# Attention in a graph network: the difference "product minus group maximum" formed by TensorE in PSUM instead of by VectorE in SBUF

## The chip, the cores and the metric

The kernel runs on one core of a Trainium2 chip, in one launch. The metric is the device time of that launch in microseconds (us), the median of several runs. The engines are called TensorE (PE in the rows; PEld are its weight loads), VectorE (DVE), ScalarE (ACT), GpSimd (POOL) and SyncE (SP). SBUF is the working memory of 128 partitions, PSUM the eight banks of 128 x 512 f32 into which TensorE writes.

## The reference

Four graph layers over 6250 nodes and 206,250 edges (sorted by destination) are applied one after the other to node rows x of 16 numbers. The change touches the fourth, an attention over the edges of each node:

```python
w_m = (efeat @ W_msg + b_msg).reshape(E, in_f, -1)      # 16 x 16 per edge
w_a = (efeat @ W_attn + b_attn).reshape(E, in_f, -1)
h_src = feat[src][:, :, None]
e1 = w_m * h_src
e2 = w_a * h_src
seg_max = jax.ops.segment_max(e2, dst, num_segments=N)
ex = jnp.exp(e2 - seg_max[dst])
denom = jax.ops.segment_sum(ex, dst, num_segments=N)
attn = ex / denom[dst]
ft = jax.ops.segment_sum(e1 * attn, dst, num_segments=N)
return ft.sum(axis=1)
```

## The kernel before

The fourth layer puts the edges of a node into quads of four; an edge that is missing is marked void. Each of the 128 partitions owns 440 quads (LQ), worked through in 110 blocks (NBQ) of QB = 4 quads, so a block holds 16 edges per partition. For each edge there are CH = 256 attention products and 256 message products. `walk` runs the first blocks unrolled, then a loop of two blocks per turn, then the last ones unrolled. The engines are ordered by semaphores written out by hand; `At(k)` is block k, `at.of(per, more)` a semaphore count for it, `turn_wait` a wait. Each engine works strictly in the order of its own program:

- SyncE loads the lines of two quads of each block and stores `S`, the maxima first (`keep_tops`, L2097 to L2099, when `s_sub` says so), the sums later (L2107).
- GpSimd gathers the 16 source rows of a block into `got` (L2127) and the lines of the other two quads (L2138).
- TensorE, in `step` (L2199): for block k it makes the matrices of block k+1, `matrices(at, q, half)` (L2171, L2178), two matmuls of K = 32 rows per half quad in different row groups, into PSUM `pw[half]`; the sums over the four edges of a quad of block k-1, `quad_sum` (L2181, L2186), four accumulating matmuls of the identity with `X[:, q, n, :]`, into `pq[q % 2]`; and the transposes of the lines of block k+2, `turned` (L2160, L2167), into `pturn`. The order in a step: matrices of quad 0, quad sums 0 and 1, matrices of quads 1 to 3, transposes, quad sums 2 and 3.
- VectorE, in `a_block` (L2299): `times` (L2272, L2281) multiplies `pw[half]` by the gathered row into `T[at.b]` (attention and message products of half a quad). For block k it takes the maximum over the four edges of each quad (L2324, L2327), carries it forward over the quads of the same node (`forward`, L2304) and back (`back`, L2309), each step depending on the one before. Between these steps stand the `times` of block k+1 (`ahead`) and the additions of quad sums of block k-1 to the running state (`add`, L2287, L2294). Then come the two subtractions of the maxima from `T` in place, one for each half of the block (L2343), each followed by `s_sub`; `drop` (L2345, L2346), the last `times`, two additions, the two products of `X` and the message part (L2356, waiting for `s_x`), and `carried` (L2359).
- ScalarE, in `step` (L2236): marks of void edges (L2230), the two exponentials from `T` to `X` (L2243) after `s_sub` and the quad sums of the block before (`X` is one buffer), the exponential of `drop` (L2245), the copy of the transposed lines from PSUM to `efT` (`features`, L2234), and indices (L2226).

`S[b]` holds maxima, sums and weighted sums of four quads. All of this is f32.

## Time and profile before

| what | value |
|---|---|
| median of 3 runs | 10060.28 us |
| lowest and highest | 10052.39, 10067.98 us |
| span of the profiled execution | 13003.9 us |
| in it, VectorE busy | 8219.9 us (63%) |
| TensorE busy | 8950.8 us (69%) |
| GpSimd busy | 6780.0 us (52%) |
| ScalarE busy | 2527.0 us (19%) |
| mean granted TensorE clock | 0.763 of full speed |

The profile is one execution with the hardware profiler on. The span is the time from its first to its last instruction; no other time of that execution is recorded. It is 2944 us longer than the median of the runs without a profile, so stretches of it are compared with each other, not with the median. Shares over the whole span mix four layers with different limits; what the change is worth is read in the loop of the fourth. A TensorE record of an f32 matmul is one of two; each has a weight load of its own. The clock is 1.00 at full speed (2.4 GHz), 0.50 at half of it (1.2 GHz).

### The profile page before, as it was taken

Reading aid. Unit: us, or ns where it says so; the run is one execution under the profiler, and the core shown is the slowest. Engines: PE = TensorE matmul, PEld = TensorE weight load, DVE = VectorE, ACT = ScalarE, POOL = GpSimd, SP = SyncE. Lnnn points to the kernel's source line nnn. Section 1 sums busy time; section 2 is a strip of 40 time slices with the busy share of each in tenths; the row PEclk is TensorE's granted clock in tenths of the full one; section 3 lists DMA queues with packets and bytes.
Section 4 is the critical chain, followed back from the end, with each engine's and each line's share of the span. In section 5 each row is a group of like instructions: output and inputs, shape, how many; then the busy total and the mean of one; then the engine's idle time right before and its main releaser. Section 6 shows DMA issues by size and latency. Waiting matters only on the chain. (4 is left out here: it accounts for less than half of the span.)

```text
span 13003.9 us, 142499 instructions
## 1 busy us (share of the span) xinstructions
PE 8950.8 (69%) x38162; PEld 4441.1 (34%) x38162; DVE 8219.9 (63%) x14849; ACT 2527.0 (19%) x4281; POOL 6780.0 (52%) x6455
## 2 busy tenths in 40 slices
PE   2776773777777771666666666666488888888885
PEld 2333431333333330333333333334233333333332
DVE  7444442555555552555555555566488988889888
ACT  7443441111011010111111111111011111111112
POOL 0554554334443435444444444444377777777775
PEclk9887885777766765777777777778688888888887
DMA  1111111111111101100010000000122222222223
GB/s 69 41 44 38 41 42 21 26 27 25 27 27 25 26 23 15 19 19 17 19 19 19 18 19 18 18 18 12 23 65 65 65 65 65 65 66 68 65 65 107
DMA packets 495922, 492.95 MB, mean 38 GB/s; under 512 B 179009, under 2 KB 394840, under 8 KB 494937
## 3 DMA queue, kind: packets, MB, share of 16 engines
q1 hardware_dynamic: 298201, 371.17, 8.7%
q0 software_dynamic: 197504, 119.78, 6.0%
q14 instruction: 189, 1.55, 0.0%
q8 instruction: 28, 0.46, 0.0%
HBM read 240.53 MB, written 249.95 MB: 38 GB/s over the span
## 5 line engine op out<-in xcount | busy, mean ns | idle before, releaser
L1688 PE MATMUL sheaf_acc<-sheaf_hot_hi,sheaf_wide 128*128 128x392 bf16 x9672 | 2145.8, 376 | 1144.1 <-issue 627.8
L1608 POOL DMA_INDIRECT sheaf_got<-tab,sheaf_idx x1612 | 1664.6, 1033 | 2091.5 <-DVEq L1969 1607.4
L2127 POOL DMA_INDIRECT attn_got<-tab,attn_line x1760 | 2393.3, 1360 | 604.2 <-issue 557.4
L2186 PE MATMUL attn_q<-attn_X,ident 128*128 128x512 f32 x3520 | 1835.0, 681 | 9.3 <-DVE attn_X L2356 8.6
L1688 PEld LDWEIGHTS sheaf_acc<-sheaf_hot_hi,sheaf_wide 128*128 128x128 bf16 x9672 | 1015.4, 113 | 2062.4 <-issue 1668.0
L1862 DVE TENSOR_SCALAR sheaf_hot_hi<-sheaf_number,src_hi 128x784 bf16<-128x784 f16 x1612 | 684.7, 425 | 1421.8 <-remote 1125.8
L2178 PE MATMUL attn_w<-src_hi 32*128 32x512 f32 x3520 | 1120.8, 826 | 524.1 <-ACT src_hi L2234 317.7
L1213 POOL DMA_INDIRECT nnconv_got<-tab,nnconv_idx x1116 | 1058.2, 948 | 370.3 <-issue 322.2
L2281 DVE TENSOR_TENSOR attn_T<-attn_w,attn_got 128x1024 f32<-128x1024 f32 x880 | 1055.4, 1220 | 247.3 <-DMA attn_got<-tab,attn_line 175.3
L2186 PEld LDWEIGHTS attn_q<-attn_X,ident 128*128 128x128 f32 x3520 | 767.7, 225 | 1019.9 <-issue 1019.9
L788 PE MATMUL gcn_acc<-gcn_hot,pieces 128*128 128x512 bf16 x3906 | 974.9, 403 | 96.1 <-issue 91.5
L705 POOL DMA_INDIRECT gcn_got<-tab,gcn_idx x868 | 848.0, 977 | 308.0 <-issue 273.2
L1381 DVE TENSOR_TENSOR nnconv_prod<-nnconv_w,nnconv_got 128x1024 f32<-128x1024 f32 x434 | 489.3, 1145 | 801.1 <-remote 580.7
L1242 PE MATMUL nnconv_w<-nnconv_W,nnconv_tT 64*128 64x256 f32 x3224 | 707.9, 561 | 345.2 <-DVE nnconv_prod L1381 178.6
L1255 PE MATMUL nnconv_acc<-nnconv_hot,pieces 128*128 128x512 bf16 x2604 | 672.1, 415 | 224.8 <-issue 123.3
L2178 PEld LDWEIGHTS attn_w<-src_hi 32*128 32x128 f32 x3520 | 340.6, 224 | 1202.6 <-issue 1202.6
L2243 ACT ACTIVATE attn_X<-attn_T 128x2048 f32<-128x2048 f32 x220 | 420.4, 1911 | 1687.6 <-DVEq L85 1086.0
L733 DVE SCALAR_TENSOR_TENSOR gcn_held<-gcn_blk,blk_of,gcn_acc 128x512 f32<-128x512 f16 x186 | 138.8, 746 | 922.7 <-remote 629.2
L1242 PEld LDWEIGHTS nnconv_w<-nnconv_W,nnconv_tT 64*128 64x128 f32 x3224 | 444.7, 273 | 686.1 <-issue 633.4
L1313 ACT ACTIVATE nnconv_tT<-nnconv_t 64x416 f32<-64x416 f32 x496 | 253.9, 512 | 2151.7 <-PE nnconv_t L1231 2106.5
L1210 POOL COPY nnconv_idx<-srci 128x18 int32 (+1 forms) x62 | 12.4, 200 | 1249.0 <-DVEq L85 1162.9
L788 PEld LDWEIGHTS gcn_acc<-gcn_hot,pieces 128*128 128x128 bf16 x3906 | 394.1, 105 | 600.2 <-issue 243.6
(444 smaller groups left out, 12592.1 us busy)
## 6 DMA issues: line engine op xcount, KB each, us to landing
states<-attn_S SPq DMA_DIRECT2D x110, 1024.0 KB, 4.2
states<-attn_S SPq DMA_DIRECT2D x110, 512.0 KB
attn_got<-tab,attn_line POOLq DMA_INDIRECT x1760
sheaf_got<-tab,sheaf_idx POOLq DMA_INDIRECT x1612
gcn_key<-src_key SPq DMA_DIRECT2D x62, 384.0 KB
gcn_blk<-src_blk SPq DMA_DIRECT2D x62, 384.0 KB
nnconv_got<-tab,nnconv_idx POOLq DMA_INDIRECT x1116
nnconv_key<-src_key SPq DMA_DIRECT2D x62, 256.0 KB
```

What stands on the lines that cost most here:

```text
L705: e.indirect_dma_start(out=got[at.b][:, j, :], out_offset=None, in_=tab[0], in_offset=indices(idx[at.b], j)).then_inc(s_got[at.b], 16)
L788: mm = e.matmul(pacc[q][:, :], pieces[:, part, n * NBLK:(n + 1) * NBLK, :].rearrange("p b f -> p (b f)"), hot[q][:, n, :], start=n + part ...
L1213: e.indirect_dma_start(out=got[at.b][:, j, :], out_offset=None, in_=tab[1], in_offset=indices(idx[at.b], j)).then_inc(s_got[at.b], 16)
L1242: mm = [e.matmul(to[:, t * 512 + (j - 2 * g) * 256:t * 512 + (j - 2 * g + 1) * 256], tT[at.b][t * H1:(t + 1) * H1, j * P:(j + 1) * P], W2[ ...
L1255: mm = e.matmul(pacc[:, :], pieces[:, part, n * NBLK:(n + 1) * NBLK, :].rearrange("p b f -> p (b f)"), hot[q][:, n, :], start=n + part == ...
L1608: e.indirect_dma_start(out=got[at.b][:, j, D:D + T2], out_offset=None, in_=tab[2], in_offset=indices(idx[at.b], j)).then_inc(s_got[j // JH ...
L1688: mm = e.matmul(pacc[k][:, 0:HH], wide[at.b][half][:, part, col, :], hot_hi[(at.b * J + j) % NR][:, k * HH:(k + 1) * HH], start=False, sto ...
L1862: e.tensor_scalar(hot_hi[(at.b * J + j) % NR][:, :], number[:, :], src_hi[:, bass.ds(at.of(J, j), 1)], None, ALU.is_equal).then_inc(s_hot, 1)
L2127: e.indirect_dma_start(out=got[at.b][:, 4 * q + n, :], out_offset=None, in_=tab[3], in_offset=indices(ids[:, q, n, :], D + 2)).then_inc(s_ ...
L2178: e.matmul(pw[half][:, n * 512:(n + 1) * 512], efT[at.b][r0:r0 + RW, q, :], Wc[r0:r0 + RW, :], start=True, stop=True).then_inc(s_col[n], 1)
L2186: mm = e.matmul(pq[q % 2][:, :], ident[:, :], X[:, q, n, :], start=n == 0, stop=n == 3)
L2281: e.tensor_tensor(T[at.b][:, q, 2 * half:2 * half + 2, :].rearrange("p n (i o) -> p (n i) o", o=D), pw[half].rearrange("p (i o) -> p i o", ...
```

## The change

The group maxima are no longer subtracted on VectorE. For each half quad, TensorE multiplies the attention products in `T` by the identity into a PSUM bank and adds in the same bank the maxima of the quad multiplied by a negated identity `neg` (read twice through a broadcast): `below`. ScalarE takes the exponential from that bank to `X`, half a quad at a time, eight instead of two. Two banks `pr` are used in turn (`ring`, `ring_free`), the transposes of the lines take one of their slots. The quads go through in the order 3, 2, 1, 0, in which `back` finishes their maxima; VectorE releases them one by one with `s_fin`, and makes the products of `X` quad by quad in the same order. TensorE's order in a step becomes: matrices of quad 0, quad sums 0 and 1, matrices of quad 1, quad sums 2 and 3, half a quad of matrices (2,0), transposes, then the four quads of `below` with one half quad of matrices after each of the first three. ScalarE copies the transposed lines ahead of the exponentials. VectorE spreads its `times` by half quads over the maximum steps, and adds quad sums 0 and 1 after the forward steps 0 and 1.

```diff
...
-            pturn = ps("attn_turn", [P, 512], banks)
-            s_w, s_v, s_one, s_turn, s_ef, s_t, s_prod, s_quad, s_taken, s_sub, s_e, s_x, s_state = seml(
-                "w", "v", "one", "turn", "ef", "t", "prod", "quad", "taken", "sub", "e", "x", "state")
+            pr = [ps(f"attn_r{q}", [P, 512], banks) for q in range(2)]
+            neg = sb("attn_neg", [P, P], c=banks)
+            s_w, s_v, s_one, s_turn, s_ef, s_t, s_prod, s_quad, s_taken, s_fin, s_below, s_e, s_x, s_scale, s_state = seml(
+                "w", "v", "one", "turn", "ef", "t", "prod", "quad", "taken", "fin", "below", "e", "x", "scale", "state")
...
-            halves = (slice(0, QB // 2), slice(QB // 2, QB))
+            NX = 2 * QB
+            def ring(at, n):
+                return pr[(at.k + n) % 2 if at.k < NBQ - 2 else (n + 1) % 2]
+            def ring_free(e, at, n):
+                if n == 0 and at.k > 0:
+                    turn_wait(e, s_x, at.of(NX, -1))
+                if n in (1, 2) and at.k >= NBQ - 2:
+                    turn_wait(e, s_x, at.of(NX, n - 2))
+                elif n == 1 and at.k > 0:
+                    turn_wait(e, s_x, at.of(NX, 0))
+                elif n < 3 and (n == 2 or at.k == 0):
+                    turn_wait(e, s_ef, at.of(1, n + 2))
+                elif n >= 3:
+                    turn_wait(e, s_x, at.of(NX, n - 2))
...
-                        turn_wait(e, s_sub, at.of(2, 1))
+                        turn_wait(e, s_fin, at.of(QB, QB))
...
-                    def turned(at):
+                    def turned(at, to):
...
-                        turn_wait(e, s_ef, at.of(1, 1))
                         for q in range(QB):
-                            mm = e.transpose(pturn[:, q * P:(q + 1) * P], line[at.b][:, q, :, :].rearrange("p n f -> p (n f)"),
+                            mm = e.transpose(to[:, q * P:(q + 1) * P], line[at.b][:, q, :, :].rearrange("p n f -> p (n f)"),
...
-                        turn_wait(e, s_prod, at.of(2, q // 2 + 1))
+                        turn_wait(e, s_prod, at.of(QB, QB - q))
...
-                    def quad_matrices(at, q):
-                        if at.k < NBQ:
-                            for half in range(2):
-                                matrices(at, q, half)
-                    def quad_sums(at, half):
-                        if at.k >= 0:
-                            for q in range(QB // 2):
-                                quad_sum(at, QB // 2 * half + q)
+                    def below(at, q):
+                        turn_wait(e, s_fin, at.of(QB, QB - q))
+                        for half in range(2):
+                            n = 2 * (QB - 1 - q) + half + 1
+                            ring_free(e, at, n)
+                            to = ring(at, n)[:, :].rearrange("p (n c) -> p n c", n=2)
+                            e.matmul(to, ident[:, :], T[at.b][:, q, 2 * half:2 * half + 2, 0:CH], start=True, stop=False)
+                            e.matmul(to, neg[:, :], S[at.b][:, q, None, 0:CH].to_broadcast([P, 2, CH]),
+                                     start=False, stop=True).then_inc(s_below, 1)
                     def step(at):
-                        quad_matrices(at.plus(1), 0)
-                        quad_sums(at.plus(-1), 0)
-                        for q in range(1, QB):
-                            quad_matrices(at.plus(1), q)
+                        nxt, prev = at.plus(1), at.plus(-1)
+                        more, before = nxt.k < NBQ, prev.k >= 0
+                        for q in range(2):
+                            if more:
+                                for half in range(2):
+                                    matrices(nxt, q, half)
+                            if before:
+                                for n in range(2):
+                                    quad_sum(prev, 2 * q + n)
+                        if more:
+                            matrices(nxt, 2, 0)
                         if at.k < NBQ - 2:
-                            turned(at.plus(2))
-                        quad_sums(at.plus(-1), 1)
-                    turned(At(0))
+                            ring_free(e, at, 0)
+                            turned(at.plus(2), ring(at, 0))
+                        for n, q in enumerate(range(QB - 1, -1, -1)):
+                            below(at, q)
+                            if more and n < 3:
+                                matrices(nxt, 2 + (n + 1) // 2, (n + 1) % 2)
+                    turned(At(0), pr[0])
...
-                    turned(At(1))
+                    turned(At(1), pr[1])
...
-                    e.sem_inc(s_x, 3)
+                    e.sem_inc(s_scale, 1)
...
-                    def features(at):
+                    def features(at, of):
                         e.wait_ge(s_turn, at.of(1, 1))
-                        e.copy(efT[at.b].rearrange("p q n -> p (q n)"), pturn[:, :]).then_inc(s_ef, 1)
+                        e.copy(efT[at.b].rearrange("p q n -> p (q n)"), of[:, :]).then_inc(s_ef, 1)
...
-                        for n, half in enumerate(halves):
-                            e.wait_ge(s_sub, at.of(2, n + 1))
+                            features(at.plus(2), ring(at, 0))
+                        for q in range(QB - 1, -1, -1):
                             if at.k > 0:
-                                e.wait_ge(s_quad, at.of(QB, QB // 2 * (n + 1) - QB))
-                            e.activation(X[:, half, :, 0:CH], T[at.b][:, half, :, 0:CH], ACT.Exp).then_inc(s_x, 1)
+                                e.wait_ge(s_quad, at.of(QB, q + 1 - QB))
+                            for half in range(2):
+                                n = 2 * (QB - 1 - q) + half + 1
+                                e.wait_ge(s_below, at.of(NX, n))
+                                e.activation(X[:, q, 2 * half:2 * half + 2, 0:CH], ring(at, n)[:, :].rearrange("p (n c) -> p n c", n=2),
+                                             ACT.Exp).then_inc(s_x, 1)
                         e.wait_ge(s_e, at.of(1, 1))
-                        e.activation(scale[:, :], drop[:, :], ACT.Exp).then_inc(s_x, 1)
-                        if at.k < NBQ - 2:
-                            features(at.plus(2))
+                        e.activation(scale[:, :], drop[:, :], ACT.Exp).then_inc(s_scale, 1)
...
-                    features(At(0))
+                    features(At(0), pr[0])
                     marks(At(1))
-                    features(At(1))
+                    features(At(1), pr[1])
...
+                    ch.do(e.tensor_scalar(neg[:, :], ident[:, :], -1.0, None, ALU.mult))
...
-                                e.wait_ge(s_prod, at.of(2, -2))
+                                e.wait_ge(s_prod, at.of(QB, -QB))
...
-                        for q, cols in enumerate((((0, 0), (0, 1)), ((1, 0), (1, 1)), ((2, 0),), ((2, 1),))):
+                        for q, col in enumerate(((0, 0), (0, 1), (1, 0), (1, 1))):
                             n = forward(q)
-                            ahead(*cols)
+                            ahead(col)
+                            if q < 2:
+                                add(q)
                             ch.wait(n)
-                        n = back(2)
-                        add(0)
-                        ch.wait(n)
-                        n = back(1)
-                        ahead((3, 0))
-                        ch.wait(n)
-                        back(0)
-                        add(1)
-                        ch.sync()
-                        for half in halves:
-                            to = Tb[:, half, :, 0:CH]
-                            ch.do(e.tensor_tensor(to, to, Sb[:, half, None, 0:CH].to_broadcast([P, QB // 2, 4, CH]), ALU.subtract))
-                            ch.tell(s_sub)
+                        e.sem_inc(s_fin, 1)
+                        for q, col in ((2, (2, 0)), (1, (2, 1)), (0, (3, 0))):
+                            n = back(q)
+                            ahead(col)
+                            ch.wait(n)
+                            e.sem_inc(s_fin, 1)
...
+                        add(2)
                         ahead((3, 1))
-                        add(2)
...
-                        for n, half in enumerate(halves):
-                            e.wait_ge(s_x, at.of(3, 3 + n + 1))
-                            e.tensor_tensor(X[:, half, :, CH:], Tb[:, half, :, CH:], X[:, half, :, 0:CH],
-                                            ALU.mult).then_inc(s_prod, 1)
-                        e.wait_ge(s_x, at.of(3, 6))
+                        for q in range(QB - 1, -1, -1):
+                            e.wait_ge(s_x, at.of(NX, 2 * (QB - q)))
+                            e.tensor_tensor(X[:, q, :, CH:], Tb[:, q, :, CH:], X[:, q, :, 0:CH], ALU.mult).then_inc(s_prod, 1)
+                        e.wait_ge(s_scale, at.of(1, 2))
...
-                    walk(e, NBQ, a_block, ch, 2 + QB + QB - 1 + 2 + 2 + 1, head=4)
+                    walk(e, NBQ, a_block, ch, 2 + QB + QB - 1 + 2 + 1, head=4)
...
```

## Rows read from the trace of the kernel before

**Rows 1.** Head of the page of the profile.

```profile
span 13003.9 us, 142499 instructions
```

**Rows 2.** Busy time of each engine in the attention loop (columns in the first line).

```profile
core 0: us, PE busy (x) PEld busy (x) DVE busy (x) ACT busy (x) POOL busy (x), PEclk, DMA share, GB/s
9341.60:12893.60 3552.00, 3035.58 (x7468) 1183.60 (x7468) 3165.19 (x3079) 539.13 (x656) 2628.07 (x2071) 0.82 0.21 65
```

**Rows 3.** Instructions of line 2359, one per block; ns min/median/max, first and last start.

```profile
L2359 DVE TENSOR_TENSOR src_lo<-attn_S,src_lo x110: 678/684/687, 9392.9 to 12879.8; 128x512 f32<-128x512 f32 x110
```

**Rows 4.** VectorE groups by line, attention loop: count, busy us, mean ns, idle before.

```profile
L2281 DVE TENSOR_TENSOR attn_T<-attn_w,attn_got 128x1024 f32<-128x1024 f32 x880 | 1055.4, 1220 | 247.3 <-DMA attn_got<-tab,attn_line 175.3 <-DVE src_lo L2346 33.0 <-PE attn_w L2178 30.8
L2343 DVE TENSOR_TENSOR attn_T<-attn_T,attn_S 128x2048 f32<-128x2048 f32 x220 | 503.5, 2289 | 16.9 <-DVE attn_T L2343 12.9 <-issue 3.1
L2356 DVE TENSOR_TENSOR attn_X<-attn_T,attn_X 128x2048 f32<-128x2048 f32 x220 | 494.4, 2289 | 24.8 <-DVE attn_S L2294 21.1 <-issue 3.0
```

**Rows 5.** Waits of VectorE, attention loop: us in total, times, longest.

```profile
DVE attn_T L2281 <- DMA attn_got<-tab,attn_line: 175.3, 93, 33.1
```

**Rows 6.** TensorE in order of time, one block: start, us, instructions, idle before.

```profile
10999.56 1.64 PE L2178 MATMUL attn_w<-src_hi 32*128 32x512 f32 x8 [3.11 <-ACT src_hi L2234]
11001.13 8.52 PE L2186 MATMUL attn_q<-attn_X,ident 128*128 128x512 f32 x16
11011.99 2.26 PE L2178 MATMUL attn_w<-src_hi 32*128 32x512 f32 x8 [2.34 <-issue]
11014.65 3.20 PE L2178 MATMUL attn_w<-src_hi 32*128 32x512 f32 x8 [0.40 <-DVE attn_T L2281]
...
11021.74 1.11 PE L2167 MATMUL attn_turn<-ident,attn_line 128*128 128x128 f32 x4
```

**Rows 7.** TensorE weight loads in the middle of a quad sum.

```profile
11004.34 0.19 PEld L2186 LDWEIGHTS attn_q<-attn_X,ident 128*128 128x128 f32 x1 [0.24 <-issue]
11004.77 0.19 PEld L2186 LDWEIGHTS attn_q<-attn_X,ident 128*128 128x128 f32 x1 [0.24 <-issue]
```

**Rows 8.** TensorE, products of one half-group alone.

```profile
11011.99 1.13 PE L2178 MATMUL attn_w<-src_hi 32*128 32x512 f32 x4 [2.34 <-issue]
```

**Rows 9.** Stretches of that block; columns as in Rows 2, PEclk third from the end.

```profile
11001.10:11009.70 8.60, 8.55 (x18) 3.50 (x16) 6.07 (x5) 0.00 (x0) 7.08 (x6) 0.83 0.15 42
11011.90:11014.10 2.20, 2.11 (x8) 0.66 (x8) 2.20 (x3) 0.20 (x1) 0.21 (x1) 1.00 0.25 80
11014.20:11022.60 8.40, 7.64 (x22) 2.98 (x21) 7.58 (x12) 0.00 (x0) 6.47 (x7) 0.50 0.06 10
```

**Rows 10.** VectorE in order of time, the next block's beginning.

```profile
11032.16 4.50 DVE L2356 TENSOR_TENSOR attn_X<-attn_T,attn_X 128x2048 f32<-128x2048 f32 x2 [0.23 <-DVE attn_S L2294]
11036.57 0.68 DVE L2359 TENSOR_TENSOR src_lo<-attn_S,src_lo 128x512 f32<-128x512 f32 x1
11037.79 2.31 DVE L2324 TENSOR_TENSOR attn_two<-attn_T 128x2048 f32<-128x2048 f32 x1 [0.54 <-DVE src_lo L2359]
11040.23 1.23 DVE L2327 TENSOR_TENSOR attn_S<-attn_two 128x1024 f32<-128x1024 f32 x1
11041.61 0.48 DVE L2305 SCALAR_TENSOR_TENSOR attn_S<-attn_S,apart_q 128x256 f32<-128x256 f32 x1 [0.16 <-DVE attn_S L2327]
11042.57 2.36 DVE L2281 TENSOR_TENSOR attn_T<-attn_w,attn_got 128x1024 f32<-128x1024 f32 x2 [0.48 <-DMA attn_got<-tab,attn_line]
11044.84 0.48 DVE L2305 SCALAR_TENSOR_TENSOR attn_S<-attn_S,apart_q 128x256 f32<-128x256 f32 x1
```

**Rows 11.** VectorE, the first addition of a quad sum and what follows it.

```profile
11019.90 0.74 DVE L2294 SCALAR_TENSOR_TENSOR attn_S<-src_lo,same_q,attn_q 128x512 f32<-128x512 f32 x1
11020.56 0.48 DVE L2310 SCALAR_TENSOR_TENSOR attn_S<-attn_S,apart_q 128x256 f32<-128x256 f32 x1
```

**Rows 12.** ScalarE in order of time, the same block.

```profile
11030.61 1.91 ACT L2243 ACTIVATE attn_X<-attn_T 128x2048 f32<-128x2048 f32 x1 [3.09 <-PE attn_q L2186]
...
11032.73 0.57 ACT L2234 COPY src_hi<-attn_turn 128x512 f32<-128x512 f32 x1
```

## The prediction

> **What bounds the kernel now.** I first read which part the change touches: only the loop over quad blocks, 9341.6 to 12893.6 us of the profiled execution, 3552 of 13 003.9 us [rows 1, 2]. Line 2359 runs once per block, 110 times; first and last start are 9392.9 and 12 879.8, so a block takes (12879.8 - 9392.9) / 109 = 32.0 us [rows 3]. Then the engines: VectorE is busy 3165 of 3552 us, TensorE 3036, GpSimd 2628, ScalarE 539 [rows 2]. By this row VectorE sets the pace (28.8 us of each 32.0) and TensorE is close behind. VectorE's longest outside wait is for the gathered rows, 175.3 us, of which 33.1 is one wait [rows 5], at the loop's start as I take it, so 142 us or 1.3 us a block. The rest of its idle time is short waits on its own results.
>
> Third, I asked whether TensorE's 86% is real, because its ends are modelled. Weight loads in the middle of a quad sum start 0.43 us apart (11004.34, 11004.77) while one takes 0.19 [rows 7]. Each f32 matmul of 512 columns is two such pairs of records: a quad sum of four matmuls is 8 records, 8 x 0.427 = 3.41 us, and the four of a block 13.7 us. That is streaming time, not slack: 16 records took 8.52 us in the block shown [rows 6], where the granted clock was 0.83, a mixture of the full 2.4 GHz and the half [rows 9].
>
> **What goes.** VectorE's two subtractions of 2.29 us in each block (L2343) [rows 4]. With them goes one semaphore round; about 4.6 us a block, if VectorE is what the loop waits for.
>
> **What is split.** The two products of 2.29 us (L2356) become four of half the size. Two run in 4.50 us [rows 10]. Half-size instructions of that width run as pairs in 2.36 us, so they start (2.36 - 1.22) = 1.14 us apart [rows 4, 10]; four take 3 x 1.14 + 1.22 = 4.6 us. That costs 0.1 us. On ScalarE two exponentials of 1.91 us become eight of 512 elements from PSUM. The nearest row is its copy of 512 elements from PSUM, 0.57 us [rows 12]; as bounds I take that and 1.91 / 4 = 0.48 for the slope alone plus 0.2; 0.6 each, 4.8 us a block. ScalarE is busy 4.9 us a block [rows 2] and has 27 to spare and only the last one stands near a chain. The removed copy order (features before the exponentials now) is covered by the same slack, and so is the one-time building of the negated identity.
>
> **What is added.** Eight half groups, each two f32 matmuls of 512 columns over the full array: 32 records. No record of before is a subtraction through the negated identity, but the quad sum has its shape in everything (128 rows, identity weights, 512 f32 columns). 32 x 0.427 = 13.7 us at the full clock [rows 7]. The bound below is one pass instead of two, 0.21 us a record, 6.8 us; no row shows such a pace for f32, so I take the upper value. Above, the half clock would double it, 27 us; the low clock is weighed further down.
>
> **TensorE's own sum per block afterwards.** 64 full records, 27.3 us. Products of efT and Wc: a half group alone took 1.13 us to its modelled end [rows 8], the following one started after the same 1.13 us (2.26 for both) [rows 6]; followed by something other than itself I count 1.0. Of the eight, two pairs can still start together (1.6 us for four matmuls [rows 6], which began at the full clock), four stand alone between other work: 2 x 1.6 + 4 x 1.0 = 7.2. Transposes 0.7 (0.91 between their start at 11021.74 and the next burst, at the half clock [rows 6, 9]; half of that would be the floor). Sum 35.2 us. This is already 3.2 us over the present block. TensorE becomes the bound.
>
> **The chain round one block.** An engine's sum is a floor; the order of the queues decides. I walk one block from the end of its predecessor's last product (time 0), durations from the rows, 0.2 us for a semaphore between engines.
> - TensorE had to wait for time 0, because quad sum 0 comes first in its queue and product 0 is now the last made. Quad sums 0 and 1 end at 0.2 + 6.8 = 7.0. The half (1,0) ends at 8.0.
> - The half (1,1) needs the T of (0,1). VectorE: carried sum 0.8 and loop turn 0.2, pair maxima 2.3 (L2324 at 11037.79, the next at 11040.23), maxima 1.4, to 4.7 [rows 10]; forward 0.4, times 1.14, add 0.66 (L2294 to the next start), forward 0.4, times 1.2 gives 8.5 [rows 10, 11]. TensorE waits from 8.0 to 8.65 and ends at 9.65.
> - Quad sums 2 and 3 to 16.5, half (2,0) to 17.5, transposes to 18.2. The forward maxima are ready by 12, so the subtraction isn't held up by them.
> - Three quads subtracted, each 3.41, and three halves of 1.0 between them: 18.2 + 13.2 = 31.4. Here half (3,1) is made. The second releases (maxima group by group) come from VectorE several us ahead of their use, since VectorE itself is waiting for halves (2,0), (2,1), (3,0).
> - VectorE then makes T of (3,1): 31.4 + 0.2 + 1.14, adds 0.74, and a wait on its own result 0.23 [rows 10]: 33.7. Only now do the four products stand next in its queue: 33.7 + 4.6 = 38.4. The last exponential is ready sooner: TensorE finishes quad 0 at 31.4 + 3.4 = 34.8, plus 0.2 and 0.6 gives 35.6, and product 0 begins at 37.1. TensorE meanwhile makes the next block's first pair, to 36.4, and stands idle for 2 us.
>
> So the block takes 38.4 us at the full clock. The stall that the subtractions were is replaced by TensorE's queue, and what is late next is the row of four products behind half (3,1).
>
> **The clock.** In the block shown, after a gap of 3.11 us in which TensorE did nothing, the burst that followed took 8.52 instead of 6.83 us, so 1.7 us were lost; after a gap of 2.34 us the next 2.2 us ran at 1.00; in the sparse stretch of single halves it was 0.50 for 8.4 us [rows 6, 9]. My gap of 2.2 us is like the second, and the sparse stretch is now filled. If the loss of 1.7 us occurs, 0.7 of it lies in the wait for T of (0,1), and 1.0 remains: 39.4. I take 38.6.
>
> **A rule of the skill on the split pairs.** The rows: a pair of halves took 1.64 us as eight records, a single half 1.13 [rows 6, 8]. The Trainium skill (TensorE: Matmul & The Clock Gate, section "Measured speedup vs the span model") has four row tiles of K=32 run concurrently at 3.07 times the speed of one after the other. The change now separates two of the four pairs of a block by full-array work, which that rule speaks against. Estimated from that page, four matmuls in 1.1 us would make the pairs left intact 1 us a block cheaper than my sum.
>
> **The sum.** 38.6 - 32.0 = 6.6 us a block x 110 = +726 us on the profiled execution, 13 004 to about 13 730. The runs without a profile have a median of 10 060 us, 2944 less; the rows can't say where. In this loop little of it can lie: VectorE's busy time alone is 28.8 of 32.0 us a block. What may be missing in an unprofiled run is the wait for gathers, at most 142 us, which would make the loop of before shorter but not that of after, whose gathers have a longer block to hide in (GpSimd is busy 2628 / 110 = 24 us a block [rows 2]). I take half, 71. 10 060 + 726 + 71 = 10 857, call it 10 850.
>
> **Rivals.**
> - A, the forecast: TensorE's queue plus the tail of four products, 38.4 to 39.4 us a block and 0 to 142 us for the gathers: 10 764 to 11 016. For it: every record price is seen. Chance 0.70.
> - B, the clock falls twice a block or for longer: another 1.7 us, 41.1 us: 10 060 + 9.1 x 110 = 11 061. For it: the clock was 0.82 over the whole loop [rows 2]. Against it: TensorE's gaps shrink. 0.12.
> - C, TensorE's own work sets the pace and the tail is hidden, because T of (3,1) comes sooner than I walked: 35.2 us, 10 060 + 3.2 x 110 = 10 412. Against it: product 0 is last on VectorE and first for TensorE. 0.10.
> - D, faster: the added records lie beside the others as TensorE's idle time allows, VectorE stays the bound and loses 4.6 - 0.1 = 4.5 us a block: 10 060 - 495 = 9565. Its place is the eight subtractions; by my chain it breaks even when a new record costs 0.427 - 6.6 / 32 = 0.22 us. For it: weight loads fill only 1184 of 3552 us [rows 2]. Against it: their spacing is 0.43 us whatever they take [rows 7]. 0.05. The Trainium skill (Perfetto Trace Analysis, section "Identifying the Most-Contended Engine") judges TensorE's headroom by the busy share of weight loads, here 33%, and not by matmul busy time; by that rule there is room. In f32 the trace speaks otherwise.
> - E, a mixture near the break-even of D: no measurable change, 0.03.
>
> **How the numbers follow.** The likeliest case gives 10 850. To leave out no more than 2 in 10 the range must take in A and most of B, and a part of the way to C: 10 600 to 11 070. Faster by over 0.2% is D, 0.05; within 0.2%, about what a measurement of this kernel can tell from no change, E, 0.03; slower A, B and C, 0.92.
>
> **What would show it.** In the profile of the changed kernel: line 2359's successor at a spacing of 38 to 39 us; the records of the subtraction 0.43 us apart; TensorE over 90% busy with a gap of about 2 us ahead of quad sum 0; VectorE below 27 us a block, waiting for TensorE at the T products; no wait for gathers. Wrong would be: a spacing of the new records near 0.2 us (D); products on VectorE that start before T of (3,1) (C); a clock under 0.8 in the loop (B).

## The result, and the profile after

The changed kernel takes 10869.6 us (median of 4 runs, 10866.1 to 10872.3) against 10061.6 us for the kernel before (median of 4 of its runs on those chips): a ratio of 1.0804, 95% interval 1.0792 to 1.0817. It is 808 us slower, and the forecast was 10850.

Two lines of its page: the span, and the granted TensorE clock in 40 slices of it, in tenths (the attention loop is the last 16).

```profile
span 10867.0 us, 152955 instructions
...
PEclk9999967888886799999999969999999999999997
```

The span is 10867 us, close to the runs, where that of the kernel before was 13 004 [rows 1]; what is known of that difference comes at the end. Busy time in the attention loop, and the instruction that runs once a block (count, ns min/median/max, first and last start):

```profile
core 0: us, PE busy (x) PEld busy (x) DVE busy (x) ACT busy (x) POOL busy (x), PEclk, DMA share, GB/s
6434.00:10740.00 4306.00, 4028.17 (x10911) 1568.76 (x10910) 2669.84 (x3057) 654.17 (x1313) 2000.77 (x2046) 0.98 0.18 53
```

```profile
L2385 DVE TENSOR_TENSOR src_lo<-attn_S,src_lo x110: 681/684/687, 6455.3 to 10738.2; 128x512 f32<-128x512 f32 x110
```

A block takes (10738.2 - 6455.3) / 109 = 39.3 us; it was 32.0 [rows 3]. That the loop took 32.0 us a block in the runs of 10 060 us too is worked out below, under the gathers. TensorE is busy 94% of the loop at a clock of 0.98 (before: 85% at 0.82), VectorE 62% (before: 89%) [rows 2]. The difference, 7.3 x 109 = 796 us, is all but 12 us of the result.

One block on TensorE, in order of time (start, us, instructions, idle time before them and what ended it):

```profile
8818.40 8.80 PE L2203 MATMUL attn_q<-attn_X,ident 128*128 128x512 f32 x16 [2.48 <-DVE attn_X L2383]
8827.13 1.14 PE L2195 MATMUL attn_w<-src_hi 32*128 32x512 f32 x8
8828.20 7.13 PE L2203 MATMUL attn_q<-attn_X,ident 128*128 128x512 f32 x16
8835.26 1.13 PE L2195 MATMUL attn_w<-src_hi 32*128 32x512 f32 x4
8836.32 0.66 PE L2184 MATMUL attn_r<-ident,attn_line 128*128 128x128 f32 x4
8836.82 1.02 PE L2213 MATMUL attn_r<-attn_T,ident 128*128 128x512 f32 x2
8837.68 1.02 PE L2214 MATMUL attn_r<-attn_S,attn_neg 128*128 128x512 f32 x2
...
8849.72 1.13 PE L2195 MATMUL attn_w<-src_hi 32*128 32x512 f32 x4
...
8854.41 1.14 PE L2195 MATMUL attn_w<-src_hi 32*128 32x512 f32 x8
8858.05 7.10 PE L2203 MATMUL attn_q<-attn_X,ident 128*128 128x512 f32 x16 [2.49 <-DVE attn_X L2383]
```

The block begins with the quad sums at 8818.40 and the next at 8858.05. The differences run in pairs of records (L2213 the products, L2214 the maxima) that start 0.86 us apart, so 0.43 a record; between them stand the single halves (L2195), 1.06 us each from their start to the next start. At the end TensorE makes the next block's first pair (8854.41) and then stands idle for 2.49 us, until product 0 is made. VectorE in the same block:

```profile
8836.54 1.22 DVE L2313 TENSOR_TENSOR attn_T<-attn_w,attn_got 128x1024 f32<-128x1024 f32 x1 [4.99 <-PE attn_w L2195]
...
8850.99 1.23 DVE L2313 TENSOR_TENSOR attn_T<-attn_w,attn_got 128x1024 f32<-128x1024 f32 x1 [1.74 <-PE attn_w L2195]
8852.14 0.74 DVE L2326 SCALAR_TENSOR_TENSOR attn_S<-attn_S,same_q,attn_q 128x512 f32<-128x512 f32 x1
8853.02 4.63 DVE L2383 TENSOR_TENSOR attn_X<-attn_T,attn_X 128x1024 f32<-128x1024 f32 x4 [0.15 <-DVE attn_S L2326]
```

T of (2,0) waits 4.99 us for its half, and T of (3,1) 1.74 us. Only behind T of (3,1) and the last addition come the four products, 4.63 us, and they end when TensorE may go on. The exponentials from PSUM are not what the products wait for: in the whole loop VectorE waited for one four times, 9.9 us together. Each takes 0.60 us:

```profile
8814.88 0.60 ACT L2275 ACTIVATE attn_X<-attn_r 128x512 f32<-128x512 f32 x1 [1.12 <-PE attn_r L2214]
```

The waits of the loop in total (us, times, longest), and the two quad-sum bursts of two successive blocks with their granted clock, third from the end:

```profile
DVE attn_T L2313 <- PE attn_w L2195: 1432.6, 427, 5.4
...
PE attn_q L2203 <- DVE attn_X L2383: 264.0, 106, 2.5
```

```profile
8818.40:8827.10 8.70, 8.70 (x16) 3.52 (x16) 7.66 (x8) 0.20 (x1) 5.82 (x6) 0.80 0.09 21
8858.00:8865.10 7.10, 7.05 (x18) 2.98 (x18) 6.31 (x7) 0.20 (x1) 3.65 (x5) 1.00 0.09 21
```

The first burst lasted 8.7 us at 0.80, the second 7.1 at 1.00. So the second burst ran at full speed and the first in part at the low clock. Of the 108 blocks that can be compared, 58 begin with such a slowed burst (8.6 to 8.7 us to the next start) and take 39.6 us in the mean; the other 50 take 39.1 (39.0 or 39.4).

### The profile page after: what moved, and what is told of

It reads as the page before. It is cut to its first block and busy times, and to the rows that moved or that the text cites. A ratio compares the mean times of both kernels' runs of the same rounds, so it can differ in the third digit from the quotient of the medians.

```text
span 10867.0 us, 152955 instructions
## 1 busy us (share of the span) xinstructions
PE 9177.5 (84%) x41682; PEld 4488.1 (41%) x41682; DVE 7781.9 (72%) x14850; ACT 2641.3 (24%) x4941; POOL 6341.7 (58%) x6455
## 5 line engine op out<-in xcount | busy, mean ns | idle before, releaser
L1688 PE MATMUL sheaf_acc<-sheaf_hot_hi,sheaf_wide 128*128 128x392 bf16 x9672 | 1918.1, 348 | 342.2 <-DVE sheaf_hot_hi L1862 341.8
L2145 POOL DMA_INDIRECT attn_got<-tab,attn_line x1760 | 1697.3, 964 | 572.4 <-issue 556.5
L2203 PE MATMUL attn_q<-attn_X,ident 128*128 128x512 f32 x3520 | 1663.5, 628 | 273.7 <-DVE attn_X L2383 273.7
L2156 POOL DMA_INDIRECT attn_line<-in_lines,attn_line_at x220 | 275.5, 1252 | 1502.7 <-ACT attn_line_at L2255 1468.6
L2213 PE MATMUL attn_r<-attn_T,ident 128*128 128x512 f32 x1760 | 934.0, 612 | 0.0
L2214 PE MATMUL attn_r<-attn_S,attn_neg 128*128 128x512 f32 x1760 | 899.0, 592 | 0.0
L2275 ACT ACTIVATE attn_X<-attn_r 128x512 f32<-128x512 f32 x880 | 525.6, 597 | 1435.0 <-PE attn_r L2214 1435.0
L2195 PE MATMUL attn_w<-src_hi 32*128 32x512 f32 x3520 | 809.6, 646 | 37.2 <-DVE attn_T L2313 35.3
L1242 PE MATMUL nnconv_w<-nnconv_W,nnconv_tT 64*128 64x256 f32 x3224 | 525.2, 471 | 9.0 <-DVE nnconv_prod L1381 5.3
L2383 DVE TENSOR_TENSOR attn_X<-attn_T,attn_X 128x1024 f32<-128x1024 f32 x440 | 509.7, 1220 | 30.5 <-DVE attn_S L2326 19.9
```

What stands on the lines that cost most here:

```text
L1688: mm = e.matmul(pacc[k][:, 0:HH], wide[at.b][half][:, part, col, :], hot_hi[(at.b * J + j) % NR][:, k * HH:(k + 1) * HH], start=False, sto ...
L2145: e.indirect_dma_start(out=got[at.b][:, 4 * q + n, :], out_offset=None, in_=tab[3], in_offset=indices(ids[:, q, n, :], D + 2)).then_inc(s_ ...
L2195: e.matmul(pw[half][:, n * 512:(n + 1) * 512], efT[at.b][r0:r0 + RW, q, :], Wc[r0:r0 + RW, :], start=True, stop=True).then_inc(s_col[n], 1)
L2203: mm = e.matmul(pq[q % 2][:, :], ident[:, :], X[:, q, n, :], start=n == 0, stop=n == 3)
L2213: e.matmul(to, ident[:, :], T[at.b][:, q, 2 * half:2 * half + 2, 0:CH], start=True, stop=False)
L2214: e.matmul(to, neg[:, :], S[at.b][:, q, None, 0:CH].to_broadcast([P, 2, CH]), start=False, stop=True).then_inc(s_below, 1)
```

## Experiments

The runs fell on three chips, each used on one occasion. On one of them the kernel before takes 10048 us, as in the result (`after_here`, `one_matmul_load`, `early_half_load`, `no_subtract`); on the two others it takes 13 015 and 13 037 us (all other runs), though its attention loop takes 32.0 us a block there. I call these two kinds of chips; whether the chip or the occasion makes the difference isn't shown. So totals are compared only with the kernel before on the same chip, and loops by the spacing of the once-a-block instruction, as long as the increments described in the last section weren't late in it.

**The changed kernel again (`after_here`).** No edit.

> The changed kernel, unchanged, on a chip of the kind where the kernel before takes about 13020 us. There TensorE's semaphore increments were seen to arrive late while GpSimd issues gathers without a break, and the needless VectorE work in vector_load, which halts GpSimd for some us, was there with the loop at 39.32 us a block. If the late increments are what lengthened the loops of tail and early_half (44 us), this kernel too takes 42 to 45 us a block here, 14150 to 14500 us, and was slower without the needless work than with it. If they come from what those two changed, this one takes 39.3 us a block and about 13840 us.

It ran on a chip of the first kind: 10862 us against 10048, ratio 1.081 (1.079 to 1.083), 39.3 us a block. That repeats the result. What it takes on the other kind of chip, which the expectation was about, stays open.

**Giving VectorE its work back (`vector_load`).**

```diff
                             n = back(q)
+                            if q == 2:
+                                for _ in range(2):
+                                    ch.to(e.tensor_tensor(two[:, :, :, :], Tb[:, :, 0:2, 0:CH], Tb[:, :, 2:4, 0:CH], ALU.max))
                             ahead(col)
```

> The changed kernel with 4.6 us of needless VectorE work a block (twice the 128x2048 maximum into a scratch tile) put where VectorE waits 5.0 to 5.4 us for the half (2,0). It gives back to VectorE just the time that the subtractions took. Theory, VectorE is not what the loop waits for there: 0 to 0.3 us a block, 10870 to 10900 us. Rival, VectorE still sets the pace: 4.6 x 110 = 506 us more, about 11375 us.

```profile
L2388 DVE TENSOR_TENSOR src_lo<-attn_S,src_lo x110: 680/683/742, 9421.9 to 13708.2; 128x512 f32<-128x512 f32 x110
```

(13708.2 - 9421.9) / 109 = 39.3 us a block, as without the added work. The total, 13 860 us, can't be set beside 10 870, since the chip was of the other kind. VectorE waited for no late increment in this loop. 4.6 us of VectorE work a block cost nothing: in the changed kernel VectorE is not the pace. The changed kernel itself wasn't run on this kind of chip, so the two loops compared here are of different chips; but `early_half_load`, below, carries the same added work on the chip of `after_here`, and its moved half gains all that was expected of it.

**One step moved: the half (3,1) earlier (`early_half_load`).** With the added work of `vector_load` kept, so that it is compared with that loop.

```diff
-                            if more and n < 3:
-                                matrices(nxt, 2 + (n + 1) // 2, (n + 1) % 2)
+                            if more and n == 0:
+                                matrices(nxt, 2, 1)
+                            if more and n == 1:
+                                matrices(nxt, 3, 0)
+                                matrices(nxt, 3, 1)
```

> early_half (half (3,1) right behind (3,0)) with the same needless VectorE work, again against vector_load's 39.32 us a block. Theory, chain with the tail of products: 1.85 us less, 37.4 to 37.5 us. Rival, TensorE's own work alone: 1.0 us less, 38.2. Rival, the place of the half costs nothing: 39.3.

The once-a-block instruction; then T of (3,1) and the products:

```profile
L2391 DVE TENSOR_TENSOR src_lo<-attn_S,src_lo x110: 681/683/686, 6451.9 to 10537.1; 128x512 f32<-128x512 f32 x110
```

```profile
8509.29 1.22 DVE L2316 TENSOR_TENSOR attn_T<-attn_w,attn_got 128x1024 f32<-128x1024 f32 x1
...
8511.31 4.63 DVE L2389 TENSOR_TENSOR attn_X<-attn_T,attn_X 128x1024 f32<-128x1024 f32 x4 [0.15 <-DVE attn_S L2329]
```

(10537.1 - 6451.9) / 109 = 37.5 us, 1.8 less; in total 10 659 us, 203 us less than `after_here` on the same chip (ratios to the kernel before 1.061, 1.059 to 1.063, against 1.081). T of (3,1) at 8509.29 no longer waits. TensorE's saving alone would have been 1.0, and its idle time ahead of the quad sums fell from 2.5 to 1.9 us. The clock is not behind the gain: blocks with a slowed burst take 37.8 us here (39.6 in the changed kernel), and 55 of 109 bursts are slowed, as many as there. The tail of products is on the loop, as the forecast's chain had it.

**Half of the added matmuls (`one_matmul_load`).** The matmul of the negated maxima is left out (the exponentials are then of the products alone), VectorE's added work is kept.

```diff
-                            e.matmul(to, ident[:, :], T[at.b][:, q, 2 * half:2 * half + 2, 0:CH], start=True, stop=False)
-                            e.matmul(to, neg[:, :], S[at.b][:, q, None, 0:CH].to_broadcast([P, 2, CH]),
-                                     start=False, stop=True).then_inc(s_below, 1)
+                            e.matmul(to, ident[:, :], T[at.b][:, q, 2 * half:2 * half + 2, 0:CH],
+                                     start=True, stop=True).then_inc(s_below, 1)
```

> one_matmul (second matmul of each half left out) together with the needless 4.6 us of VectorE work of vector_load, to be compared with vector_load alone (39.32 us a block, 13860 us). Theory, TensorE's queue sets the pace: 16 x 0.427 = 6.8 us less a block, 32.5. Rival, the eight steps through PSUM and ScalarE set it: 38 to 39. If increments are still late: over 40.

The once-a-block instruction; then TensorE and VectorE at the end of one block:

```profile
L2387 DVE TENSOR_TENSOR src_lo<-attn_S,src_lo x110: 680/683/686, 6447.8 to 10233.9; 128x512 f32<-128x512 f32 x110
```

```profile
8530.63 1.13 PE L2195 MATMUL attn_w<-src_hi 32*128 32x512 f32 x4
8531.69 1.98 PE L2213 MATMUL attn_r<-attn_T,ident 128*128 128x512 f32 x4
8533.60 1.14 PE L2195 MATMUL attn_w<-src_hi 32*128 32x512 f32 x8
8538.93 3.72 PE L2203 MATMUL attn_q<-attn_X,ident 128*128 128x512 f32 x5 [4.19 <-DVE attn_X L2385]
```

```profile
8531.90 1.23 DVE L2312 TENSOR_TENSOR attn_T<-attn_w,attn_got 128x1024 f32<-128x1024 f32 x1
...
8534.01 4.63 DVE L2385 TENSOR_TENSOR attn_X<-attn_T,attn_X 128x1024 f32<-128x1024 f32 x4 [0.23 <-DVE attn_S L2325]
```

(10233.9 - 6447.8) / 109 = 34.7 us: 4.6 less, 500 us in all (10 362 against 10 862), not 6.8. The rival of the PSUM path is out (38 to 39). The rows show what the expectation left out. Half (3,1) is made at 8530.63, ahead of the last quad's differences (8531.69). The tail of VectorE hangs on that half: T at 8531.90, products to 8538.6. So the last quad's four records lie beside the tail, and only 12 of the 16 are on the loop: 12 x 0.427 = 5.1. In their place TensorE is idle 4.19 us. The 0.5 us missing from these 5.1 went to the clock. Here the first burst is slowed in every block, in the changed kernel in 58 of 108. Blocks whose burst took 8.7 us take 34.6 us here and 39.6 there, which is 5.0 less, close to the 5.1 of 12 records; and in 22 blocks the burst took 10.0 us and the block 35.9.

**VectorE's relief by itself (`no_subtract`).** The kernel before with its subtractions left out (the exponentials are of the unsubtracted products).

```diff
                         for half in halves:
-                            to = Tb[:, half, :, 0:CH]
-                            ch.do(e.tensor_tensor(to, to, Sb[:, half, None, 0:CH].to_broadcast([P, QB // 2, 4, CH]), ALU.subtract))
                             ch.tell(s_sub)
```

> The kernel before with its two subtractions a block left out and nothing put in their place (exponentials of the unsubtracted products). It prices the relief of VectorE by itself. As the prediction had it (VectorE alone sets the pace): 4.6 us less a block, 32.0 to 27.4, 506 us less. New theory from the traces, GpSimd's gathers fill the block of before as well (16 x (1.36 + 0.34) + 2 x (1.06 + 0.3) + 2.1 = 32.0 us, the 1.36 being lengthened by VectorE's large instructions): it falls only as far as GpSimd's issue does, to 28.5 to 30.5 us, 170 to 385 us less. If neither is the pace: 32.0.

The once-a-block instruction; then VectorE, TensorE and ScalarE at the end of a block:

```profile
L2357 DVE TENSOR_TENSOR src_lo<-attn_S,src_lo x110: 681/684/686, 6437.6 to 9780.4; 128x512 f32<-128x512 f32 x110
```

```profile
8523.33 0.75 DVE L2294 SCALAR_TENSOR_TENSOR attn_S<-attn_S,same_q,attn_q 128x512 f32<-128x512 f32 x1 [1.57 <-PE attn_q L2186]
8526.75 0.75 DVE L2294 SCALAR_TENSOR_TENSOR attn_S<-attn_S,same_q,attn_q 128x512 f32<-128x512 f32 x1 [2.68 <-PE attn_q L2186]
8527.73 4.49 DVE L2354 TENSOR_TENSOR attn_X<-attn_T,attn_X 128x2048 f32<-128x2048 f32 x2 [0.23 <-DVE attn_S L2294]
```

```profile
8517.92 1.11 PE L2167 MATMUL attn_turn<-ident,attn_line 128*128 128x128 f32 x4
8518.83 7.79 PE L2186 MATMUL attn_q<-attn_X,ident 128*128 128x512 f32 x16
8529.73 1.76 PE L2178 MATMUL attn_w<-src_hi 32*128 32x512 f32 x8 [3.11 <-ACT src_hi L2234]
```

```profile
8526.65 1.91 ACT L2243 ACTIVATE attn_X<-attn_T 128x2048 f32<-128x2048 f32 x1 [5.80 <-PE attn_q L2186]
...
8528.77 0.57 ACT L2234 COPY src_hi<-attn_turn 128x512 f32<-128x512 f32 x1
```

(9780.4 - 6437.6) / 109 = 30.7 us; in total 9908 against 10 048 us, ratio 0.986 (0.984 to 0.988). So 4.6 us of VectorE work taken away are worth 1.3 us a block. The rows show the wait in its place: TensorE's quad sums 2 and 3 begin at 8518.83, behind the transposes; their additions on VectorE wait for them (1.57 and 2.68 us), and the products stand behind the additions. TensorE in turn waits 3.11 us for ScalarE's copy of the transposed lines, which stands behind the second exponential, and that one waits for the quad sums. So here the pace is a circle of TensorE and ScalarE. It is there in the kernel before too, with the same 3.11 us [rows 6, 12]. The change also moved this copy ahead of the exponentials; what that is worth by itself was not run.

The new theory, of the gathers, missed its range by 0.2 us, since this circle comes first. But GpSimd had no time left in the loop before, and has some here. Its gathers before, then its wait for ScalarE's indices here, both in 2500 us of the loop (count, busy us, mean ns, idle before):

```profile
L2127 POOL DMA_INDIRECT attn_got<-tab,attn_line x1248 | 1704.3, 1366 | 423.5 <-issue 393.9 <-DVE attn_T L2281 29.0 <-PE attn_turn L2167 0.6
```

```profile
L2138 POOL DMA_INDIRECT attn_line<-in_lines,attn_line_at x163 | 376.0, 2307 | 237.8 <-ACT attn_line_at L2226 212.8 <-issue 25.0
```

Before, GpSimd waited for other engines for 30 of 2500 us, the 29.0 and 0.6 of the first line; here it waits 213 us for ScalarE alone, and a gather's issue takes 0.98 us in the mean instead of 1.37. So the block before was full on GpSimd as well as nearly full on VectorE. That holds for the profiled chip; there is no profile of the kernel before on the other kind.

**Sharing the difference between the two engines (`shared`).** TensorE forms it for quads 3 and 2, VectorE for 0 and 1; the longer edit changes the order of four engines. Its core on VectorE:

```diff
+                        to = Tb[:, 0:2, :, 0:CH]
+                        ch.do(e.tensor_tensor(to, to, Sb[:, 0:2, None, 0:CH].to_broadcast([P, 2, 4, CH]), ALU.subtract))
+                        ch.tell(s_sub)
...
+                        product(slice(0, 2), 3)
+                        product(slice(3, 4), 2)
+                        product(slice(2, 3), 5)
```

and on TensorE:

```diff
+                        pair(0)
+                        sums_of(0, 1)
+                        pair(1)
+                        sums_of(2, 3)
+                        pair(2)
+                        if at.k < NBQ - 2:
+                            ring_free(e, at, 0)
+                            turned(at.plus(2), ring(at, 0))
+                        below(at, 3)
+                        pair(3)
+                        below(at, 2)
```

> A version of its own: TensorE forms the difference for quads 3 and 2 only, VectorE subtracts in one instruction of 2.29 us for quads 0 and 1, whose products come first, so that TensorE starts the quad sums while VectorE still makes the other two; TensorE makes the halves in pairs, VectorE the first T of the next block ahead of its maxima. Theory, the loop before is VectorE's and the loop after is TensorE's: TensorE has 64 - 16 = 48 full records of 0.427 us, four pairs of 1.1 and 0.5 for the transposes, 25.4 us; VectorE about 24.3 + 2.3 us busy and 1.5 to 2 of waits, 28 to 29.5 us a block against 32.0: 9700 to 9800 us where the kernel before takes 10060. Rival, the order and the handing over between three engines cost and not one engine's work: at or above the kernel before.

The once-a-block instruction, and GpSimd's groups in 2500 us of the loop (count, busy us, mean ns, idle before):

```profile
L2408 DVE TENSOR_TENSOR src_lo<-attn_S,src_lo x110: 679/683/685, 9428.1 to 12894.5; 128x512 f32<-128x512 f32 x110
```

```profile
L2146 POOL DMA_INDIRECT attn_got<-tab,attn_line x1253 | 1702.7, 1359 | 425.3 <-issue 424.3 <-DVE attn_T L2323 1.0
L2157 POOL DMA_INDIRECT attn_line<-in_lines,attn_line_at x158 | 150.9, 955 | 55.9 <-issue 47.5 <-ACT attn_line_at L2261 8.4
L2163 POOL TENSOR_TENSOR attn_line<-attn_line,void_src 128x8 int32<-128x8 int32 x79 | 16.4, 208 | 151.0 <-DMA attn_line<-in_lines,attn_line_at 151.0
```

(12894.5 - 9428.1) / 109 = 31.8 us against 32.0; the ratio of the totals is 0.999 (0.996 to 1.001), no difference. Neither TensorE's 25 us nor VectorE's 28 were reached. All of GpSimd's time lies in these groups (busy and idle add up to 2502 us). The idle part is the 0.3 us from one issue to the next and the wait for its own lines, but for 9 us. So GpSimd has no free time in this loop on this kind of chip, as in the loop before. That this held `shared` at 31.8 us is argued, not tested, and some increments were late here too (84 us of such waits in 2500). It was not run on the other kind of chip.

**Runs whose loops the late increments lengthened.** `tail` put VectorE's products of quads 3 and 2 ahead of T of (3,1), `early_half` is the moved half without the added VectorE work, `one_matmul` (twice) the kernel with one matmul and without that work, `no_matmul` has neither matmul.

> The changed kernel with VectorE's order alone changed: products of quads 3 and 2 ahead of T(3,1) and the last addition. TensorE's program is untouched. Theory, product 0 is the last on VectorE and the first thing that TensorE needs: it ends 1.25 us earlier, TensorE's gap falls from 2.5 to 1.2 us: 10870 - 137 = about 10730 us, to 10705 if the clock no longer falls. Rival, TensorE's own work sets the pace and the gap is a symptom: 10870, no change.

> The changed kernel with one TensorE group moved: half (3,1) right behind half (3,0) instead of one quad of differences later. Theory, chain with the tail: the two together take 1.1 instead of 2.1 us on TensorE, and VectorE no longer meets T(3,1) late, so the last product ends 1.85 us earlier: 10870 - 1.85 x 110 = about 10670 us, ratio to the kernel before 1.06. Rival, TensorE's own work alone (no tail): only the 1.0 us, about 10755. Rival, the split costs nothing: 10870.

> The changed kernel without the second of the two matmuls per half quad (the negated maxima are left out, so the exponentials are of the products alone). Theory, TensorE's queue sets the pace: 16 records fewer at 0.427 us each, 6.8 us less a block of 39.3, so 10870 - 751 = about 10120 us. Rival 1, the path through PSUM and ScalarE sets the pace (eight waits and exponentials instead of two): the count of matmuls matters little, over 10700 us. Rival 2, the new order of the queues (halves apart, products last first) is what costs: also over 10500 us, since it stays.

> The same kernel as one_matmul (the second matmul of each half left out). In its first run the loop took 46.1 us a block, TensorE's semaphore increments arriving up to 13 us after the matmul, and the kernel before took 13015 us on the same chip, with its loop at 32.0. Theory: the late increments belong to that chip; where the kernel before takes 10060, this one takes about 10120 (32.5 us a block). If the increments are late here again, about 46 us a block. Rival: the missing matmul itself brings the stall, and it is there with the kernel before at 10060 too.

> The changed kernel with neither of the two matmuls: TensorE only signals, ScalarE takes the exponential of the unsubtracted products from SBUF; order of all queues and the eight exponentials stay, and VectorE does no subtraction. Theory, the 32 records are the cost: 13.7 us less on TensorE, so its queue (25.6 us) falls below VectorE's work (24.3 us busy and some 2.5 us of waits on itself): about 27 us a block, 10870 - 12.3 x 110 = about 9520 us. Rival, the order costs by itself: at or above the 10060 us of the kernel before.

They took 44.0 (`tail`), 44.2, 46.2 and 46.5, and 38.3 us a block; 14 362, 14 379, 14 578 and 14 598, and 13 715 us in all, with the kernel before at 13 015 to 13 037. On the chip where `vector_load` takes 39.3 us a block, `one_matmul`, with less work on two engines, takes 46.2, which no theory of the change allows; these runs say nothing on it. `early_half` and `one_matmul` were run again in the form with the added VectorE work, above; `tail` and `no_matmul` were not. `before_again` was the kernel before once more:

> The kernel before, unchanged, for a second profile. The first profiled execution was 2944 us longer than the runs. Theory: the attention loop in it was undisturbed (32.0 us a block), the excess lies in the three layers ahead of it; then this profile shows a span near 10060 us and again 32.0 us a block. Rival: the loop was slowed too, by up to the 1.3 us a block of waits for gathers; then a block takes 30.7 to 31.5 us here and the waits are gone.

13 008 us again, and 32.0 us a block: the theory was right on the loop and wrong on the span, the rival was wrong.

## Why the prediction was right

**TensorE becomes the bound.** Right. 94% busy at 0.98, the added records 0.43 us apart as forecast [rows 7], and VectorE's time returned to it cost nothing (`vector_load`).

**TensorE's own sum.** 35.2 us were forecast. The block shown gives 35.4, with its slowed burst counted at the full clock: the 64 records take 28.5 us rather than 27.3, because a quad of differences next to a half takes 3.63 us instead of 3.41; the two pairs take 2.2 rather than 3.2, the four single halves 4.2 rather than 4.0, the transposes 0.5 rather than 0.7. So the sum is right by errors that cancel, which is luck.

**The chain.** Its steps held: `early_half_load` moved the half (3,1) and the tail of products behind it by 1.8 us a block where 1.85 was expected, and T of (2,0) waits five us for its half, which stands behind the quad sums. The lengths were too short. From the first difference to the end of half (3,1) it takes 8849.72 + 1.06 - 8836.82 = 13.96 us, where I had 13.2; two quad sums take 7.0 to 7.1 where I had 6.8; and the quad sums start 0.4 us after the last product (8853.02 + 4.63 to 8858.05) where I had 0.2. From half (3,1) to the last product it takes 6.9 us, with 7.0 forecast. So a block whose burst is not slowed takes 39.1 us, not the 38.4 of the walk.

**The clock.** I reasoned that a gap of 2.2 us on TensorE would leave the clock alone. That was wrong: the gap is 2.5 us ahead of slowed and unslowed bursts alike, and in `early_half_load`, where it is 1.9, half of the bursts are slowed too. What decides it stays open. The price was overestimated: the slowed burst loses 1.7 us, but the block only 0.5 (39.6 against 39.1), since after it the two halves of the next pair start together (8827.13, eight records in 1.07 us) and at full clock they run one after the other. Of the 0.9 us between the walk's 38.4 and the measured 39.3, 0.7 is the walk and 0.3 the clock, to within a tenth; the 38.6 that I took allowed 0.2.

**The gathers.** The step of +71 us for waits missing from an unprofiled run was wrong. The loop before takes 32.0 us a block on both kinds of chips: on the one where it takes 10 048 us in all, `no_subtract` is at 30.7 and 140 / 109 = 1.3 us lie between them, the rest of the kernel being the same. So 726 + 71 came out at 797, beside a measured 808, by two errors that cancel: a block 0.7 us too short and 71 us that do not exist. That the number is within 20 us is luck; that a block grows by about 7 us because of TensorE's queue and the tail behind it is not.

**Rival D.** It was ruled out by the spacing of the records, rightly. But its price, 495 us, was wrong in itself: `no_subtract` shows that the same relief, with nothing put on TensorE, is worth 140 us. VectorE was busiest before, at 89%, but it didn't set the pace alone. Close behind it stood the circle of quad sums, second exponential and copy, closed because `X` is a single buffer; and GpSimd, which I counted as 24 us a block of busy time, had no free time in the profiled loop.

**Pairs of halves, and the weight loads.** A pair's four matmuls occupy TensorE for 1.07 us (8827.13 to 8828.20), not the 1.6 that I took. One half alone occupies it for 1.06, so two matmuls in two row groups cost as much as four in four. The Trainium skill (TensorE: Matmul & The Clock Gate, section "Measured speedup vs the span model") gives 3.07 times for four row tiles of K=32. The row agrees: a full-array matmul of 512 columns takes 0.86 us (two records), four of them 3.4 us, and 3.4 / 1.07 is 3.2. That is an estimate, since no run has these four one after the other. Weight loads are busy 36% of the loop (1569 of 4306 us) while TensorE is the bound. The Trainium skill (Perfetto Trace Analysis, section "Identifying the Most-Contended Engine") judges headroom by that share and the share of peak arithmetic instead of matmul busy time; by the load share there would be room, and these f32 records of 0.43 us with TensorE 94% busy show none.

## What to carry to other kernels

Moving work off the busiest engine is worth only the distance to the next chain, so price the relief by leaving the work out before building its replacement: here 4.6 us a block were worth 1.3, and the replacement cost 14 us of TensorE time. An f32 matmul through an identity is no free adder: two records of 0.43 us for 512 columns. Walk the queues round one block; the last product made and the first quad sum wanted met at a point that no engine's busy share shows, and one half quad moved up took off a quarter of the loss.

## What the runs showed of the hardware

On two of the chips engines that wait for TensorE were released many us after its matmuls had ended, as if its semaphore increments arrived late. In the profile of the kernel before this is the "remote" wait of VectorE in the third layer (us in total, times, longest), 1126 us of the 2944 by which that execution was longer (two more such groups on VectorE, in the other layers, have 581 and 629):

```profile
DVE sheaf_hot_hi L1862 <- remote: 1125.8, 125, 22.2
```

In the profile of the changed kernel, from the other kind of chip, the longest wait of the same line there is for TensorE, and small:

```profile
DVE sheaf_hot_hi L1862 <- PE sheaf_acc L1688: 26.9, 58, 1.0
```

The loop of the changed kernel began at 6434 us, that of before at 9342 in its profile [rows 2], so the excess lay ahead of the attention. In the attention loop such waits appear in `one_matmul`; TensorE first, then VectorE, then ScalarE:

```profile
12006.92 1.13 PE L2195 MATMUL attn_w<-src_hi 32*128 32x512 f32 x4
12007.98 0.66 PE L2184 MATMUL attn_r<-ident,attn_line 128*128 128x128 f32 x4
12008.47 1.02 PE L2213 MATMUL attn_r<-attn_T,ident 128*128 128x512 f32 x2
12017.69 2.05 PE L2213 MATMUL attn_r<-attn_T,ident 128*128 128x512 f32 x2 [8.20 <-ACT src_hi L2262]
```

```profile
12002.81 0.48 DVE L2341 SCALAR_TENSOR_TENSOR attn_S<-attn_S,apart_q 128x256 f32<-128x256 f32 x1
12015.59 1.23 DVE L2312 TENSOR_TENSOR attn_T<-attn_w,attn_got 128x1024 f32<-128x1024 f32 x1 [12.30 <-remote]
```

```profile
12016.96 0.59 ACT L2262 COPY src_hi<-attn_r 128x512 f32<-128x512 f32 x1 [24.28 <-remote]
```

The half (2,0) was made at 12006.92 and took 1.13 us. VectorE, which at this step waits for no engine but TensorE, multiplied it at 12015.59. The transposes ended by 12008.64, ScalarE copied them at 12016.96, and TensorE, waiting for that copy, stood still for 8.20 us. In `vector_load`, on the same chip, the same step did not stall. GpSimd issued gathers without a break, one each 1.25 us, from 11999.54 until 12014.24. That the increments wait behind the gathers' traffic is argued from this, not shown, and what differs between the chips is open.

VectorE's work lengthens GpSimd's issue of a gather. On one chip its mean in the whole run is 0.965 us in `after_here` and 1.173 and 1.164 us in `early_half_load` and `one_matmul_load`, which have 4.6 us of VectorE work on 128 x 2048 f32 added to each block; beside those two instructions single issues take 3.42 and 2.02 us.
